# First stage with the chunks ahead of x and the norms behind the key products, and the last FFN unit split from PSUM

## The reference

```python
x = x + _L0_xattn_ref(_layernorm(x), ctx_4096, Wq, bq, Wk, bk)   # one head, K from ctx, values = ctx
x = x + _L0_ffn_ref(_layernorm(x), ...)                          # dense 512x512, routed low-rank part
x = x + _L1_xattn_ref(_layernorm(x), ctx_4096, mask, ...)        # 32 query heads, 8 key/value heads
x = x + _L1_ffn_ref(_layernorm(x), ...)                          # gate/up/down, 1792 wide, 4-bit weights
# _L0_xattn_ref: Q = text @ Wq.T + bq; K = features @ Wk.T + bk
#                attended = softmax(Q @ K.T / sqrt(512)) @ features
# _L1_ffn_ref:   (silu(x @ gate) * (x @ up)) @ down
```

## Time and profile before

| what | value |
|---|---|
| time, median of 3 runs | 850.12 us (850.08 to 850.28) |
| the profiled execution's own time | 850.66 us |
| its span, first to last instruction | 848.9 us |
| TensorE busy | 820.1 us, 97% of the span |
| first key product's first matmul | 6.32 us |
| first scores' first matmul | 60.96 us |
| first output transpose | 839.26 us |

### The profile page before, as it was taken

How to read it: one execution, slowest core, us unless ns; L and a number is a source line. 1 busy time by engine, 2 the same in 40 slices (tenths; PEclk the granted TensorE clock), 3 DMA queues, 4 the chain that set the end, 5 groups by cost and what they waited for, 6 DMA issues and landing times.

```text
span 848.9 us, 13289 instructions
## 1 busy us (share of the span) xinstructions
PE 820.1 (97%) x3932; PEld 671.7 (79%) x3932; DVE 564.5 (66%) x990; ACT 534.3 (63%) x1769; POOL 549.2 (65%) x554
## 2 busy tenths in 40 slices
PE   6899999999989999999999999999999999999995
PEld 5687888788778888888888888888887777777773
DVE  5605762532656666666666666666568899999996
ACT  4543461144677777777777777777677477667763
POOL 3332562321577777777777777777676268999995
PEclk9999999999999999999999999999999999999999
DMA  8510567204566666766667766667754023344302
GB/s 275 178 51 26 142 169 191 83 1 112 160 191 195 187 176 183 201 187 187 185 188 223 217 191 191 187 193 189 235 150 149 0 78 146 149 149 149 143 6 100
DMA packets 96037, 129.76 MB, mean 153 GB/s; under 512 B 25757, under 2 KB 68637, under 8 KB 95966
## 3 DMA queue, kind: packets, MB, share of 16 engines
q1 hardware_dynamic: 95966, 128.92, 51.0%
HBM read 89.82 MB, written 39.06 MB: 152 GB/s over the span
## 4 chain that ended last, share of the span: by engine, by line
PE 79%; DVE 7%; DMA 6%; ACT 2%; issue 2%; POOL 2%; SPq 1%; POOLq 0%; DVEq 0%; ACTq 0%
PE pair L1605 18%; PE pair L1607 18%; PE pair L1606 18%; PE pair L1763 8%; PE pair L1764 8%; PE pair L1857 5%; DMA land<-block_bounce 2%; DMA block_bounce<-tb 2%; SPq L577 1%; PE pair L1625 1%; DVE kv L1474 1%; DMA resid<-in_x_dram 1%; PE pair L1664 1%; PE pair L1715 1%; DVE st L1202 1%
## 5 line engine op out<-in xcount | busy, mean ns | idle before, releaser
L1605 PE MATMUL pair<-split,xnT_hi 128*128 128x512 f32 x288 | 113.3, 394 | 0.3 <-issue 0.3
L1607 PE MATMUL pair<-split,xnT_lo 128*128 128x512 f32 x288 | 112.1, 389 | 0.0
L1606 PE MATMUL pair<-split,xnT_hi 128*128 128x512 f32 x288 | 112.1, 389 | 0.0
L964 ACT ACTIVATE headT<-land,wqk 128x512 f32<-128x512 f32 x62 | 44.9, 725 | 89.9 <-DMA land<-block_bounce 65.6
L1605 PE MATMUL pair<-split,aoT_hi 128*128 128x512 f32 x244 | 95.7, 392 | 0.4 <-DVE resid L1408 0.4
L1607 PE MATMUL pair<-split,aoT_lo 128*128 128x512 f32 x244 | 95.2, 390 | 0.0
L1606 PE MATMUL pair<-split,aoT_hi 128*128 128x512 f32 x244 | 94.9, 389 | 0.0
L985 ACT ACTIVATE prob<-pair,nmax 128x128 f32<-128x128 f32 x244 | 86.0, 362 | 13.6 <-DVE nmax L1386 13.4
L1763 PE MATMUL pair<-xnT_hi,split 128*128 128x512 f32 x224 | 90.8, 405 | 2.0 <-DVE kv L1529 1.2
L739 POOL TENSOR_TENSOR prob<-prob,rinv 128x512 f32<-128x512 f32 x61 | 63.6, 1043 | 39.0 <-DVE rinv L1356 39.0
L1764 PE MATMUL pair<-xnT_lo,split 128*128 128x512 f32 x224 | 87.6, 391 | 0.0
(11 more groups left out here) (183 smaller groups left out, 2154.6 us busy)
## 6 DMA issues: line engine op xcount, KB each, us to landing
block_bounce<-tb SPq DMA_DIRECT2D x244, 128.0 KB, 2.3
land<-block_bounce SPq DMA_DIRECT2D x61, 512.0 KB, 3.4
raw<-in_wqo_dram SPq DMA_DIRECT2D x62, 256.0 KB, 3.0
kv<-in_ffn_w_dram SPq DMA_DIRECT2D x14, 768.0 KB, 4.3
kv<-in_ffn_z_dram SPq DMA_DIRECT2D x14, 768.0 KB, 5.6
kv<-key_bounce SPq DMA_DIRECT2D x32, 128.0 KB, 2.9
key_bounce<-tb SPq DMA_DIRECT2D x44, 64.0 KB, 2.0
resid<-in_x_dram SPq DMA_DIRECT2D x2, 1024.0 KB, 9.4
```

The costliest lines, as they stand in the source:

```text
L1605: pe.matmul(dst, l_hi, r_hi, start=first, stop=False)
L1606: pe.matmul(dst, l_hi, r_lo, start=False, stop=False)
L1607: return pe.matmul(dst, l_lo, r_hi, start=False, stop=last)
```

## The change

In the first stage:

- SP issues all twelve chunks first, then the first half of x, the five small loads, the second half of x.
- TensorE makes ten float32 matmuls of `ident` by itself into bank 7, whose result nobody reads, before the first key product.
- The norms have four buffers in place of two. Tiles 0 to 3 are transposed behind product 6 (when six copies are made), 4 and 5 behind product 8, 6 and 7 behind product 9. VectorE's order follows, and so do ScalarE's and GpSimd's.
- The query products (8 to 15) go by token half: first the four of half 0 (they wait for four low parts), then those of half 1 (for all eight). The scores of tiles 0 to 3 wait for 12 copies, not 15.

In the last unit:

- The product with the gate is written to the bank that it is read from, and both parts are made from there.
- ScalarE copies the down items of positions 9 and 11 ahead of `last_hi(0)`. The one of position 11 (down product 1) was VectorE's; GpSimd now adds it (`s_p1`).
- The down products are made in the order 0, 1, 2, 3, in other banks. VectorE adds all four of half 1; GpSimd has two partial additions in place of three.

```diff
@@ -260,10 +260,18 @@
+            if k == 0:
+                return (headT[:], score, prob[:], sq)[t % HALF]
...
+        def kq_item(n):
+            return (n // 2, n % 2) if n < 2 * KT else (n % KT, (n - 2 * KT) // KT)
...
+            if k == 0:
+                return bank[(4, 5, 6, 7, 4, 5, 4, 5)[t]]
@@ -386,6 +394,7 @@
         s_pb = sem("down_added_from_b")
+        s_p1 = sem("last_down_one_added")
@@ -477,10 +486,14 @@
-        LAST_DOWN = (0, 3, 1, 2)
+        LAST_DOWN = (0, 1, 2, 3)
+        LAST_SLOT = (11, 13, 10, 12)
         def last_bank(c, h):
-            return 2 * pair_of(LAST, None, ITEMS + 2 + LAST_DOWN.index(c)) + h
+            return 2 * pair_of(LAST, None, LAST_SLOT[c]) + h
+        def last_sum_bank(h):
+            return bank[2 * pair_of(LAST, None, SIDE) + h][:]
@@ -500,12 +513,13 @@
                     load(3 * k + 1 + h, ctxT[k, :, h * D:(h + 1) * D])
-                if k in (1, 2):
-                    half = slice(HALF * (k - 1), HALF * k)
-                    sp.dma_start(resid[:, half, :], x[half].rearrange("b p d -> p b d")).then_inc(s_x[k - 1], 16)
-            for dst, src in ((bias, bqk), (nw, norm_w), (mask_sb, mask), (gb, gate_b.to_broadcast([P, NR])),
-                             (gds, ffn_s)):
-                sp.dma_start(dst[:], src).then_inc(s_small, 16)
+            for h in range(2):
+                tiles = slice(HALF * h, HALF * (h + 1))
+                sp.dma_start(resid[:, tiles, :], x[tiles].rearrange("b p d -> p b d")).then_inc(s_x[h], 16)
+                if h == 0:
+                    for dst, src in ((bias, bqk), (nw, norm_w), (mask_sb, mask), (gb, gate_b.to_broadcast([P, NR])),
+                                     (gds, ffn_s)):
+                        sp.dma_start(dst[:], src).then_inc(s_small, 16)
@@ -660,13 +674,13 @@
-            for k in range(2):
+            for k in range(KT):
...
             ln_rstd(0, 0)
-            lo(3 * 2)
-            lo(3 * 3)
+            for c in range(WQ0, WQ0 + 2):
+                lo(c)
             ln_rstd(0, 1)
-            for c in range(WQ0, WFFN):
+            for c in range(WQ0 + 2, WFFN):
@@ -810,14 +824,16 @@
                 tmp, done = (tmp_a, s_pa) if c == 0 else (tmp_c, s_pb)
-                pool.wait_ge(s_ta, by_scalar(LAST, 9) + 2 + e)
+                pool.wait_ge(s_ta, by_scalar(LAST, 9) + 3 + e)
...
             pool.wait_ge(s_ta, by_scalar(LAST, 9) + 1)
+            pool.tensor_tensor(accT[:, 1, :], accT[:, 1, :], tmp_c, ALU.add).then_inc(s_p1, 1)
+            pool.wait_ge(s_ta, by_scalar(LAST, 9) + 2)
             pool.tensor_tensor(accT[:, 3, :], accT[:, 3, :], tmp_b, ALU.add).then_inc(s_pb, 1)
-            for e, (h, c) in enumerate(((0, 0), (0, 3), (1, 0))):
+            for e, (h, c) in enumerate(((0, 0), (0, 3))):
@@ -844,22 +860,19 @@
                 hi(c)
-            for t in range(2):
-                ln_hi(0, t)
-            hi(WQ0)
...
             for n in range(4 * KT):
-                m, h = (n % (2 * KT)) // 2, n % 2
+                m, h = kq_item(n)
...
                                bias=bias[:, KT * (1 - is_q) + m:KT * (1 - is_q) + m + 1]).then_inc(s_kqe, 1)
-                if n + 2 < T:
-                    ln_hi(0, n + 2)
-                if 1 <= n < KT:
-                    hi(WQ0 + n)
+                if 2 <= n < 2 + KT:
+                    hi(WQ0 + n - 2)
+                for t in {6: range(HALF), 8: (4, 5), 9: (6, 7)}.get(n, ()):
+                    ln_hi(0, t)
@@ -1176,19 +1189,22 @@
                 act.wait_ge(s_hm, UNITS + 1 + h)
-                act.activation(unit_h(LAST % 2, 0)[:, half(h)], hidden[:, half(h)], ACT.Copy).then_inc(s_hh, 1)
+                act.activation(unit_h(LAST % 2, 0)[:, half(h)], last_sum_bank(h), ACT.Copy).then_inc(s_hh, 1)
+            take(LAST, None, 9, tmp_a, down_s[:, 1 - LAST % 2, 0:1])
+            take(LAST, None, SUM, tmp_c, down_s[:, 1 - LAST % 2, 1:2])
             last_hi(0)
-            take(LAST, None, 9, tmp_a, down_s[:, 1 - LAST % 2, 0:1])
...
             act.wait_ge(s_ds, UNITS)
-            for e, (h, c) in enumerate(((0, 0), (0, 3), (1, 0))):
+            for e, (h, c) in enumerate(((0, 0), (0, 3))):
...
                     act.wait_ge(s_pa, LAST - 1)
+                else:
+                    act.wait_ge(s_p1, 1)
@@ -1216,7 +1232,9 @@
                 dve.wait_ge(s_rstd, 2 * k + group + 1)
-                if n >= 2 and k != 3:
+                if k == 0 and t >= HALF:
+                    dve.wait_ge(s_xt, n - HALF + 1)
+                elif k in (1, 2):
@@ -1235,18 +1253,23 @@
                     ctx_lo(3 * k + 1 + h)
-                if k in (1, 2):
-                    if k == 2:
-                        ln_norm(0, 0)
-                        ln_norm(0, 1)
-                    dve.wait_ge(s_x[k - 1], 16)
-                    ln_stats(0, k - 1)
+            dve.wait_ge(s_x[0], 16)
+            ln_stats(0, 0)
+            dve.wait_ge(s_x[1], 16)
+            ln_tile_stats(HALF)
+            ln_tile_stats(HALF + 1)
+            for t in range(HALF):
+                ln_norm(0, t)
+            ln_stats(0, 1, done=2)
...
             dve.tensor_tensor(wqk[:], nw[:, 0:1], nw[:, 1:2], ALU.mult).then_inc(s_wqk, 1)
-            for t in range(T):
+            ln_norm(0, HALF)
+            for t in range(HALF):
                 ln_lo(0, t)
-                if t + 2 < T:
-                    ln_norm(0, t + 2)
+            for t in range(HALF + 1, T):
+                ln_norm(0, t)
+            for t in range(HALF, T):
+                ln_lo(0, t)
@@ -1559,7 +1582,7 @@
             def last_sum(h):
-                cur = bank[2 * pair_of(LAST, None, SIDE) + h][:]
+                cur = last_sum_bank(h)
@@ -1567,25 +1590,28 @@
                 dve.wait_ge(s_si, UNITS + 1)
-                times_silu(LAST, half(h), cur, None)
+                dve.tensor_tensor(cur, cur, gated(LAST % 2)[:, half(h)], ALU.mult).then_inc(s_hm, 1)
...
                 dve.wait_ge(s_hh, UNITS + h)
-                dve.tensor_tensor(unit_h(LAST % 2, 1)[:, half(h)], hidden[:, half(h)],
+                dve.tensor_tensor(unit_h(LAST % 2, 1)[:, half(h)], last_sum_bank(h),
...
             last_lo(0)
-            take_down(LAST, None, SUM, 1, False)
...
             dve.wait_ge(s_ds, UNITS)
-            for h, c in ((0, 1), (0, 2), (1, 3), (1, 1), (1, 2)):
+            for h, c in ((0, 1), (0, 2), (1, 0), (1, 1), (1, 2), (1, 3)):
                 dve.wait_ge(s_it, item(LAST, 13) + KT * h + LAST_DOWN.index(c) + 1)
-                dve.wait_ge(s_tv, by_vector(LAST, SIDE) + 1)
+                dve.wait_ge(s_tv, by_vector(LAST, 8) + 1)
+                if c == 0:
+                    dve.wait_ge(s_pa, LAST - 1)
+                if c == 1:
+                    dve.wait_ge(s_p1, 1)
@@ -1616,6 +1642,8 @@
                     pe.wait_ge(s_xlo, n - 3)
+                elif k == 0 and t < HALF:
+                    pe.wait_ge(s_kqe, 6)
@@ -1627,8 +1655,11 @@
             pe.wait_ge(s_const, 5)
+            for _ in range(10):
+                pe.matmul(bank[7][:, tile(0)], ident[:], ident[:], start=True, stop=True)
             def kq0(n, k):
-                m, h = (n % (2 * KT)) // 2, n % 2
+                m, h = kq_item(n)
@@ -1645,21 +1676,21 @@
                     kq0(n, k)
-                    if k == KT - 2 and n in (3, 5):
-                        ln_transpose(0, n // 4)
-                    if k == KT - 1:
-                        ln_transpose(0, n + 2)
...
                     lo_done(pe, WKEY - 1)
+                    pe.wait_ge(s_xlo, HALF)
+                if n == 3 * KT:
...
                     kq0(n, k)
+                for t in {6: range(HALF), 8: (4, 5), 9: (6, 7)}.get(n, ()):
+                    ln_transpose(0, t)
...
                 if b % HALF == 0:
-                    pe.wait_ge(s_kqe, 4 * KT - 1 + b // HALF)
+                    pe.wait_ge(s_kqe, 3 * KT + KT * (b // HALF))
@@ -1992,21 +2023,21 @@
                             pe.wait_ge(s_ud, UNITS)
-                            pe.wait_ge(s_hm, UNITS + 2)
-                        elif c == 3:
-                            pe.wait_ge(s_tv, by_vector(LAST, SIDE))
+                            pe.wait_ge(s_ta, by_scalar(LAST, 9) + 1)
                         elif c == 1:
-                            pe.wait_ge(s_tv, by_vector(LAST, SIDE) + 1)
+                            pe.wait_ge(s_ta, by_scalar(LAST, 9) + 2)
+                        elif c == 2:
+                            pe.wait_ge(s_hl, LAST + 2)
                         else:
-                            pe.wait_ge(s_ta, by_scalar(LAST, 9) + 1)
+                            pe.wait_ge(s_tv, by_vector(LAST, 8) + 1)
...
                     h = t // HALF
-                    pe.wait_ge(s_tv, by_vector(LAST, SIDE) + 1 + (2, 5)[h])
-                    pe.wait_ge(s_pa, LAST + h)
+                    pe.wait_ge(s_tv, by_vector(LAST, 8) + 1 + (2, 6)[h])
+                    pe.wait_ge(s_pa, LAST)
...
```

## The result

| | before | after |
|---|---|---|
| time, median of 4 runs each | 850.2 us (850.08 to 851.52) | 842.87 us (841.65 to 843.38) |
| ratio, 95% interval | | 0.991 [0.9898, 0.9922] |
| the profiled execution: time, span | 850.66, 848.9 | 843.38, 841.6 |
| key products begin, scores begin | 6.32, 60.96 | 6.42, 54.00 |
| first partial sum of the last unit | 828.10 | 821.45 |

The forecast was 843.4, range 841.4 to 845.9. Between the two traces the span falls by 7.3 us. It can be cut at the landmarks: the start gives 60.96 - 54.00 = 6.96; from the scores to the last unit's first sum it takes 767.14 before and 767.45 after, a loss of 0.31; from there to the first output transpose 11.16 and 9.80, a gain of 1.36; from there to the end 9.64 and 10.35, a loss of 0.71. 6.96 - 0.31 + 1.36 - 0.71 = 7.30.

What follows compares the result with a forecast made beforehand. The prediction took TensorE, busy 97% of the span, as the bound, with holes at the start and in the drain. Gains of 5.7 and 1.05 us, 6.75 together, led from 850.12 to 843.4 us, range 841.4 to 845.9.

Steps and rivals of the forecast that it cites:

- The slow stretch: First key matmuls at the 1.2 GHz level lose 2.4 us; ten earlier ident products were to win back 2.0.
- Chunks ahead of TensorE: First stage: with chunks loaded before x, chunk 9 usable at 11.9, no wait left there, 2.4 us to spare.
- The wait at product 8: First query product, first to read x: TensorE waits 1.1 us for four low parts, done at 31.6.
- The rule set beside the norm: Norm of tile 4: issue order decides whether VectorE or GpSimd blocks; 1.50 us taken, VectorE first would save 1.0.
- The drain: Last unit: ScalarE's earlier copy starts GpSimd's additions sooner, GpSimd binds; gain 1.05 us, bounds 0.3 and 1.7.
- It moves along whole: Everything after the first stage is chained by semaphores with TensorE full, so it keeps the start's gain of 5.7 us.
- The sum: Whole kernel: 5.7 us from the start plus 1.05 from the drain, 6.75 us in all.
- (b): Start: the ten ident products do not shorten the slow stretch; costs 2.0 us, time 845.4, chance 0.15.
- (d): After the start: its gain is lost at a later wait with slack under 5.7 us; time 849.1, chance 0.03.
- (e): First stage: slower because x's second half lands late; landing at 31.0 gives over 851.8 us; chance 0.02.
- (f): Last unit: the new order does nothing or costs, the start's gain stays; 844.4 to 845.4 us, chance 0.10.
- (c): No wait at the first query product, or a shorter drain: up to 1.1 + 0.7 better, 841.6 to 842.3, chance 0.14.

Runs made afterwards that it cites:

- no_warmup: The changed kernel without the ten products of ident ahead of the first key product; 844.08 us, 0.9926 of before.
- rstd_later: The changed kernel with GpSimd's inverse deviations of tiles 4 to 7 one chunk later, behind chunk 14's low part; 843.40 us, 0.9918 of before.
- drain_only: The kernel before with only the last unit changed, first stage as before; 848.39 us, 0.9978 of before.
- x_first: The changed kernel with loads in the old order: halves of x ahead of chunks 6 and 9, small loads last; 848.39 us, 0.9977 of before.
- warmup_only: The kernel before with only the ten products of ident added; 850.85 us, 1.001 of before.
- start_only: The kernel before with only the first stage changed, last unit as before; 843.17 us, 0.9916 of before.

## Why the prediction was right, step by step

- **The slow stretch.** Forecast 2.0 of 2.4 gained. Measured 2.19 between no_warmup and the changed kernel. The spacing was 0.23 from the second key matmul on (0.31 before it), so no slow ones were left where I had allowed for 0.4 us.
- **Chunks ahead of TensorE.** Forecast: ScalarE gets chunk 9 at 11.9 and the norms of tiles 0 to 3 are ready at 23. In the trace ScalarE's copies of chunks 8 and 9 run from 10.99 to 12.31, the first statistics start at 15.80 (forecast 15.8), and the four norms end at 22.25. The rates summed by slice with a fixed lag gave arrival times good to about half a microsecond.
- **The wait at product 8.** Forecast 1.1, measured 0.14. This is the term that was mis-sized. The chain and its place were right (rstd_later), but I took the durations of its links from rows where the other engine worked beside them. GpSimd's two small operations took 0.20 and 1.02, not 0.56 and 1.35, VectorE being idle but for their first moments; with their starts they took 1.29, not 2.05. The low part of chunk 13 was done 0.43 sooner (24.82 for 25.25), the norm with its start took 1.46 for 1.50, and the four low parts 2.47, not 2.8, since the subtractions of one group follow each other at 0.60. Together 1.56 us: 30.04 for 31.6.
- **The rule set beside the norm.** GpSimd came first (26.08 against 26.32) and the norm was long, so the case in which VectorE is first did not come about. The same section of the Trainium skill ("SBUF — State Buffer", Who interferes with whom) says that a VectorE instruction with two inputs in SBUF contends with a GpSimd instruction that reads SBUF, and that one with at most one such input does not, outside VectorE's two-port modes. Here the subtractions from the bank took 0.72 each beside a GpSimd addition (1.45 for two at 824.24), and the one from tb had taken 1.70; the traces agree.
- **The drain.** Forecast 1.05, measured 1.36 (1.32 in drain_only). GpSimd bound it, as forecast, its five additions took 9.57 where I had 9.8 to 10.1.
- **The end.** Not in the prediction: 0.7 us lost behind the first transpose. I had taken the 9.64 us from there to the end as fixed; it was 10.35.
- **The middle.** "It moves along whole" was right within what it varies from one execution to the next.
- **The sum.** 6.75 forecast, 7.30 measured in the traces. Three errors lie in it: 1.3 too little at the start, 0.3 too little in the drain, 1.0 not foreseen behind them (0.7 at the end, 0.3 in the middle). The forecast is nearer than its terms were, and that is luck: the two gains that I took too small (1.6) and the two losses that I left out (1.0) cancel for the most part. Of the signs that I had named, the spacing, the missing gaps at chunks 6 and 9 and GpSimd as the one that releases the transposes came true; the gap of 1 us, the scores at 55.2 and the end 9.6 us behind the transposes did not. Of the rivals, (b) fell by no_warmup, (d), (e) and (f) by the landmarks. What (c) describes, no wait at product 8 and a shorter drain, is what happened, though its 841.6 to 842.3 was missed for the 1.0 us lost elsewhere. The late x of (e) came true in x_first in an unexpected form: the norms were late though x was early.

## What to carry to other kernels

Cut both traces at landmarks (the first instruction of each stage) and compare the stages; here the gains of 1.3 and the losses of 0.7 were under what the total time varies. When a queue's order is changed, follow each queue and not only the transfers: with the old order of loads the chunks came in time and the norms did not. A short wait of TensorE can be dearer than it looks, for the matmuls behind it may run at half the clock; the same warm-up gained 2.2 us without such a wait and lost 1.4 in front of one.

## What the runs showed of the hardware

- Behind a wait of TensorE of 2.5 us the granted clock was 0.52 over 3.5 us (warmup_only), behind one of 3.4 us 0.50 over 5.2 us (x_first). Behind two waits of 1.74 and 2.08 us close to each other it was 0.54 in one execution (start_only); in two others with the same last stage (before, warmup_only), behind 1.79 and 2.08 us, the products kept their 0.23 us.
- Ten float32 products of 128 columns, from 1.53 to 5.92 us, then a pause of 0.5, and the next matmul already ran at the higher level.
- Instruction transfers share the engines of the data transfers, and their moment moves with the number of instructions ahead in that engine's program. One among the stores went with a tail of 0.7 us, in which only 20 to 41 GB/s were moved, in all seven traces that had it there, and in none of the seven others. Sixteen more VectorE instructions moved it out of the stores; sixteen on GpSimd or ScalarE did not (one trace each).
